# A routed feed-forward layer on one core: gate and up products two rounds behind the turned rows, and row copies moved to ScalarE

## The reference, cut to what matters

```python
y = einsum('bct,bcd->bdt', x, weights[itok])            # 1024 tokens x 256
probs = softmax(y @ w_router); top_w, top_i = top_k(probs, 4)
top_w = top_w / sum(top_w)
g = silu(y @ we1[e]) * (y @ we3[e]) * cw[:, e]          # 16 experts, 256 -> 128
moe_out = sum_e g @ we2[e]                              # 128 -> 256
shared = silu(y @ ws1) * (y @ ws3) @ ws2                # 256 -> 512 -> 256
out = x + shared / 5 + moe_out * 4 / 5
```

## Time and profile before

| | |
|---|---|
| time of the three executions | 149.14, 149.97, 151.33 us |
| the profiled execution: its span, first to last instruction | 167.7 us |
| mean granted TensorE clock | 0.983 of full speed |
| PE (matmul) busy | 139.6 us, 83%, 816 instructions |
| PE weight loads busy | 116.3 us, 69% |
| VectorE (DVE) busy | 101.4 us, 60% |
| ScalarE (ACT) busy | 67.7 us, 40% |
| GpSimd (POOL) busy | 66.7 us, 40% |
| DMA packets | 29.81 MB in 23741 packets |
| row copies `xt<-store_t` by DMA | 43 of 128 KB each |

### The profile page before, as it was taken

How to read it: one execution, slowest core, us unless ns; L and a number is a source line. 1 busy time by engine, 2 the same in 40 slices (tenths; PEclk the granted TensorE clock), 3 DMA queues, 4 the chain that set the end, 5 groups by cost and what they waited for, 6 DMA issues and landing times.

```text
span 167.7 us, 2807 instructions
## 1 busy us (share of the span) xinstructions
PE 139.6 (83%) x816; PEld 116.3 (69%) x816; DVE 101.4 (60%) x271; ACT 67.7 (40%) x158; POOL 66.7 (40%) x79
## 2 busy tenths in 40 slices
PE   6949999898789299989979388978989499996840
PEld 2419988686578189979969377967978378884730
DVE  1304699989299365577974487473746263116993
ACT  3004379992453333263332442285333221249200
POOL 0600000027747473654847174644737467200000
PEclk9999999999999969999999999999999999999997
DMA  1724889989354635666656333533522212299433
GB/s 32 253 63 126 262 263 335 296 286 335 110 178 131 190 125 158 207 201 192 190 170 220 146 125 127 189 119 132 199 86 96 94 63 98 81 373 418 195 121 125
DMA packets 23741, 29.81 MB, mean 178 GB/s; under 512 B 4112, under 2 KB 20496, under 8 KB 23600
## 3 DMA queue, kind: packets, MB, share of 16 engines
q1 hardware_dynamic: 19632, 19.86, 35.6%
q0 software_dynamic: 3120, 8.52, 15.4%
q10 hardware_dynamic: 976, 1.26, 2.3%
HBM read 17.58 MB, written 6.42 MB: 143 GB/s over the span
## 4 chain that ended last, share of the span: by engine, by line
PE 47%; DVE 14%; DMA 14%; ACT 8%; issue 7%; another core or an unknown queue 4%; POOL 3%; DVEq 1%; POOLq 1%; ACTq 0%; SPq 0%
PE up_ps L997 15%; PE down_ps L1013 11%; PE up_ps L991 6%; PE gate_ps L950 5%; PE down_ps L975 4%; DMA store_t<-y_of,token_i 3%; DMA itok_rows<-in_itok_B 2%; POOL result L451 2%; DMA raw<-result 2%; PE down_ps L854 2%; DVE acc L809 2%; ACT raw L566 2%; ACT gt L546 2%; DMA g<-in_L_cond_weights,cond_idx 2%
## 5 line engine op out<-in xcount | busy, mean ns | idle before, releaser
L444 POOL DMA_INDIRECT store_t<-y_of,token_i x32 | 32.6, 1018 | 48.3 <-DVE token_i L709 28.2
L451 POOL DMA_INDIRECT result<-store_t,back_i x32 | 31.2, 975 | 23.7 <-DVE store_t L791 16.3
L1013 PE MATMUL down_ps<-w,gt 128*128 x94 | 25.3, 391 | 11.9 <-ACT gt L546 9.7
L1013 PEld LDWEIGHTS down_ps<-w,gt 128*128 128x128 f32 x94 | 16.1, 189 | 15.6 <-issue 14.3
L791 DVE SCALAR_TENSOR_TENSOR store_t<-down_ps,valid,store_t 128x256 f32 x47 | 21.4, 456 | 8.6 <-DVE store_t L791 3.7
L997 PE MATMUL up_ps<-w_hi,x_hi 128*128 x78 | 23.7, 304 | 1.5 <-DVE x_lo L757 0.8
L762 DVE TENSOR_TENSOR g<-sil,up_ps 128x256 f32<-128x256 f32 (+1 forms) x24 | 9.9, 412 | 20.8 <-ACT sil L554 15.6
L554 ACT ACTIVATE sil<-up_ps 128x256 f32<-128x256 f32 (+1 forms) x24 | 9.2, 384 | 32.1 <-PE up_ps L997 18.4
L997 PE MATMUL up_ps<-w_hi,x_lo 128*128 x78 | 22.0, 282 | 0.0
L997 PE MATMUL up_ps<-w_lo,x_hi 128*128 x78 | 21.9, 281 | 0.0
L546 ACT ACTIVATE gt<-down_ps 128x256 f32<-128x256 f32 (+1 forms) x24 | 9.1, 379 | 22.6 <-PE down_ps L975 12.7
(11 more groups left out here) (153 smaller groups left out, 240.5 us busy)
## 6 DMA issues: line engine op xcount, KB each, us to landing
xt<-store_t SPq DMA_DIRECT2D x43, 128.0 KB
raw<-in_L_ffn_we SPq DMA_DIRECT2D x30, 128.0 KB, 3.4
w<-in_L_ffn_we SPq DMA_DIRECT2D x4, 512.0 KB
raw<-result SPq DMA_DIRECT2D x4, 512.0 KB, 5.0
w_lo<-result SPq DMA_DIRECT2D x4, 512.0 KB, 8.1
acc<-in_x SPq DMA_DIRECT2D x2, 512.0 KB, 5.7
y_of<-store_t ACTq DMA_DIRECT2D x1, 1024.0 KB, 6.0
out<-acc SPq DMA_DIRECT2D x3, 256.0 KB, 2.1
```

The source lines that it names most:

```text
L444: pool.indirect_dma_start(xs[:, j, :], None, y_of, bass.IndirectOffsetOnAxis(ap=token_i[:, j:j + 1], axis=0),).then_inc(tile_in[j % TT], 16)
L451: pool.indirect_dma_start(result, bass.IndirectOffsetOnAxis(ap=back_i[:, j:j + 1], axis=0), merged[:, j, :], None,).then_inc(result_out[j ...
L1013: last = pe.matmul(out_ps[b][:, h, :], gt[:, b, h, :], w2_of(experts[2 + h]), start=True, stop=True)
```

## The change

Gate and up products run two rounds behind the turned rows (`UP_LAG`), the gated rows are turned four rounds behind (`TURN_LAG`) and the second products five (`LAG`), so there are 29 rounds. `x_hi` and `x_lo` get three buffers (`XB`). In rounds 2 to 5 the turn of pair i stands behind the gate and up products of pair i-2. ScalarE copies the rows of all pairs; in round i it copies those of pair i+2, last in the round before `high(n)`. SyncE keeps only the four late weight loads. The ring for copied rows moves: three places in `store_t` for pairs 0 to 5, one in `w_2` for pair 6, then three in `raw`. A turn now waits on the buffers in PSUM itself (`t_x_hi`, `t_x_lo`). Of the shared steps, `gate_up` (4,0), (5,0), (4,1), (5,1) now stand in rounds 24 to 27, ahead of the second products of that round; `gated(4)` stands on VectorE in round 28, ahead of the last merge. `item_e_i` is laid out for the new distance of 3 rounds between gate and up and the second products.

```diff
@@ -41,7 +41,11 @@
     ITEMS_UP = 2 * PAIRS
     RESULTS = T * TOP_K
     RING = 3
-    LAG = 3
+    UP_LAG = 2
+    TURN_LAG = 4
+    LAG = 5
+    XB = 3
+    XT_RAW = 5
     SRING = 4
     WARM = 8
...
+        xt_early = [store_t[:, 10 + 2 * k:12 + 2 * k, :] for k in range(RING)]
+        xt_ring = [raw[:, XT_RAW + k, :].rearrange("p (i d) -> p i d", i=2) for k in range(RING)]
+
+        def xt_of(n):
+            if n < 2 * RING:
+                return xt_early[n % RING]
+            if n == 2 * RING:
+                return w_2[:, E:E + FRONT, :]
+            return xt_ring[(n - 1) % RING]
+
+        raw_at = ([xt_early[k].rearrange("p i d -> p (i d)") for k in range(FRONT)] + [raw[:, k, :] for k in range(E - LATE)]
+                  + [xt_early[FRONT].rearrange("p i d -> p (i d)")] + [raw[:, k, :] for k in range(4)])
...
-            registers = {}
-
-            def copy_pair(n):
-
...
-                if n >= RING:
-                    sp.wait_ge(t_turned, n - RING + 1)
-                else:
-                    sp.wait_ge(dve_lo, n + 1)
-                for i in range(halves(n)):
-                    j = 2 * n + i
-                    if j < TILES:
-                        sp.wait_ge(tile_in[j % TT], 16 * (j // TT + 1))
-                    sp.dma_start(xt[:, n % RING, i, :],
-                                 xs[:, bass.ds(registers[j], 1), :].rearrange("p a d -> p (a d)")).then_inc(xt_in[n % RING], 16)
-
-            for n in range(EARLY, PAIRS):
-                copy_pair(n)
-                if n in LOAD_BEHIND:
-                    load(LOAD_BEHIND[n])
+            for n in LOAD_BEHIND:
+                sp.wait_ge(t_turned, n - RING + 1)
+                load(LOAD_BEHIND[n])
...
+            registers = {}
+
+            def copy_pair(n):
+                if n % 6 == 0:
+                    some = range(2 * n, 2 * n + 12)
+                    values = [act.alloc_register(f"tile{j}") for j in some]
+                    act.wait_ge(items_done, 1)
+                    act.load(values, item_t_i[0:1, some[0]:some[-1] + 1])
+                    registers.update({j: act.snap(v, donate=True, min_val=0, max_val=TILES - 1) for j, v in zip(some, values)})
+                if n >= RING:
+                    act.wait_ge(t_turned, n - RING + 1)
+                    if n == 2 * RING:
+                        act.wait_ge(down_done, STEPS)
+                    if n == 2 * RING + 1:
+                        act.wait_ge(t_gate_up, PLAIN)
+                        act.wait_ge(dve_lo, max(turn[XT_RAW + FRONT + k] for k in range(RING)) + 1)
+                else:
+                    act.wait_ge(dve_lo, n + 1)
+                for i in range(halves(n)):
+                    j = 2 * n + i
+                    if j < TILES:
+                        act.wait_ge(tile_in[j % TT], 16 * (j // TT + 1))
+                    act.activation(xt_of(n)[:, i, :], xs[:, bass.ds(registers[j], 1), :].rearrange("p a d -> p (a d)"), ACT.Copy).then_inc(xt_out, 1)
+
             for n in range(EARLY):
...
+                copy_pair(n)
             for n in HI_BEHIND[-1]:
                 high(n)
+            def turned_high(n):
+                if n < PAIRS:
+                    b, c, m = n % 2, n % XB, halves(n)
+                    act.wait_ge(t_turned, n + 1)
+                    act.activation((x_hi[:, c, :, :] if n >= PLAIN else x_f[b])[:, 0:m, :], xt_ps[b][:, 0:m, :], ACT.Copy).then_inc(t_x_hi, 1)
+
             for i in range(PAIRS + LAG):
                 if i == 0:
                     act.wait_ge(g_done, STEPS)
                 if i == 1:
                     act.wait_ge(down_done, STEPS)
-                if (n := pair_at(i, LAG)) is not None:
+                if i >= UP_LAG + PLAIN:
+                    turned_high(i)
+                if (n := pair_at(i, TURN_LAG)) is not None:
                     b, m = n % 2, halves(n)
                     act.wait_ge(t_g_turned, n + 1)
                     act.activation(gt[:, b, 0:m, :], gt_ps[b][:, 0:m, :], ACT.Copy).then_inc(t_g_out, 1)
-                if (n := pair_at(i, 0)) is not None:
-                    b, m = n % 2, halves(n)
-                    act.wait_ge(t_turned, n + 1)
-                    act.activation((x_hi[:, b, :, :] if n >= PLAIN else x_f[b])[:, 0:m, :], xt_ps[b][:, 0:m, :], ACT.Copy).then_inc(t_x_hi, 1)
-                if (n := pair_at(i, 1)) is not None:
+                if (n := pair_at(i, UP_LAG)) is not None:
                     b, m = n % 2, halves(n)
                     act.wait_ge(t_gate_up, n + 1)
                     act.activation(t_sil[:, b, 0:m, :], gu_ps[b][:, 0:m, 0:H], ACT.Silu).then_inc(t_silu, 1)
+                if i < UP_LAG + PLAIN:
+                    turned_high(i)
+                if i + EARLY < PAIRS:
+                    copy_pair(i + EARLY)
...
+            def turned_low(n):
+                if PLAIN <= n < PAIRS:
+                    b, c, m = n % 2, n % XB, halves(n)
+                    dve.wait_ge(t_x_hi, n + 1)
+                    dve.tensor_tensor(x_lo[:, c, 0:m, :], xt_ps[b][:, 0:m, :], x_hi[:, c, 0:m, :].bitcast(F32),
+                                      ALU.subtract).then_inc(t_x_lo, 1)
+
             tiles = []
             for i in range(PAIRS + LAG):
-                if (n := pair_at(i, 0)) is not None and n >= PLAIN:
-                    b, m = n % 2, halves(n)
-                    dve.wait_ge(t_x_hi, n + 1)
-                    dve.tensor_tensor(x_lo[:, b, 0:m, :], xt_ps[b][:, 0:m, :], x_hi[:, b, 0:m, :].bitcast(F32),
-                                      ALU.subtract).then_inc(t_x_lo, 1)
-                if (n := pair_at(i, 1)) is not None:
+                if i >= UP_LAG + PLAIN:
+                    turned_low(i)
+                if (n := pair_at(i, UP_LAG)) is not None:
                     b, m = n % 2, halves(n)
                     dve.wait_ge(t_silu, n + 1)
                     dve.tensor_tensor(t_gated[:, b, 0:m, :], t_sil[:, b, 0:m, :], gu_ps[b][:, 0:m, H:2 * H], ALU.mult).then_inc(t_g, 1)
+                if i < UP_LAG + PLAIN:
+                    turned_low(i)
                 if i < 2:
...
+                if i == PAIRS + LAG - 1:
+                    gated(STEPS)
...
+                first = UP_LAG <= i < UP_LAG + PLAIN
+                if (n := pair_at(i, 0)) is not None and n and not first:
                     turn_pair(n)
-                if i > 1:
-                    experts = load_experts(i - 1)
+                if i > UP_LAG:
+                    experts = load_experts(i - UP_LAG)
+                if (n := pair_at(i, TURN_LAG)) is not None:
+                    turn_gated(n)
+                if (n := pair_at(i, UP_LAG)) is not None:
+                    gate_up_pair(n)
+                if first:
+                    turn_pair(i)
+                if PAIRS <= i < PAIRS + 2:
+                    pe.wait_ge(dve_lo, UNITS + 1)
+                    gate_up(STEPS + i - PAIRS, 0)
+                elif PAIRS + 2 <= i < PAIRS + 4:
+                    gate_up(STEPS + i - PAIRS - 2, 1)
                 if (n := pair_at(i, LAG)) is not None:
...
-            gate_up(STEPS, 1)
-            gate_up(STEPS + 1, 0)
-            gate_up(STEPS + 1, 1)
+                    down_pair(n)
+
+            pe.wait_ge(dve_lo, UNITS + 2)
+            gate_up(STEPS + 2, 0)
             down(STEPS)
...
+            gate_up(STEPS + 2, 1)
+            gate_up(STEPS + 3, 0)
+            pe.wait_ge(t_merged, ITEMS)
+            down(STEPS + 1)
+            gate_up(STEPS + 3, 1)
+            down(STEPS + 2)
+            down(STEPS + 3)
```

The functions `turn_gated`, `gate_up_pair` and `down_pair` hold the bodies that the loop had before, with `c = n % XB` for the buffers of `x_hi` and `x_lo`. `turn_pair` gained these waits:

```diff
+                b = n % 2
+                pe.wait_ge(xt_out, 2 * n + halves(n))
                 if n < 2:
                     pe.wait_ge(silu_done, STEPS - 1 + n)
+                elif n - 2 < PLAIN:
+                    pe.wait_ge(t_x_hi, n - 1)
+                else:
+                    pe.wait_ge(t_x_lo, n - 1 - PLAIN)
```

More of the change, by code:

```diff
@@ L89, in adaln_ffn @@
         acc = sb("acc", [P, TT, D])
-        itok_rows = sb("itok_rows", [P, 1], I32)
-        quarter_i = sb("quarter_i", [P, 1], I32)
-        cond_idx = sb("cond_idx", [P, 1], I32)
+        cond_i = sb("cond_i", [P, 3], I32)
+        itok_rows, quarter_i, cond_idx = (cond_i[:, k:k + 1] for k in range(3))
         early_exp = sb("early_exp", [P, 2])
@@ L107, in adaln_ffn @@
         gt = sb("gt", [P, 2, 2, P])
-        x_hi = sb("x_hi", [P, 2, 2, D], F32R)
-        x_lo = sb("x_lo", [P, 2, 2, D], F32R)
+        x_hi = sb("x_hi", [P, XB, 2, D], F32R)
+        x_lo = sb("x_lo", [P, XB, 2, D], F32R)
         top_d = sb("top_d", [P, TT, TOP_K])
@@ L252, in adaln_ffn @@
         xt_out = sem("xt_out")
-        xt_in = [sem(f"xt_in{r}") for r in range(RING)]
         t_cleared = sem("t_cleared")
@@ L772, in _ @@
                     dve.memset(merged[:, 2 * i:2 * i + 2, :], 0.0).then_inc(t_cleared, 1)
-                if i % 6 == 1 and (first := 2 * (i - 1)) < ITEMS_UP:
+                if i % 6 == UP_LAG + 1 and (first := 2 * (i - UP_LAG - 1)) < ITEMS_UP:
```

(80 more changed lines are left out.)

28 lines of the change are left out of this document (3 added, 25 removed).

## The result

The changed kernel took 156.86 us (median of 4: 155.90 to 158.98) beside 149.69 us: ratio 1.042, 95% interval 1.034 to 1.051. The ratio compares the fast executions only, those within 1.5% of the fastest of their kernel, and so is a little under 156.86 / 149.69 = 1.048. Slower, as forecast; 155.7 was predicted, with 147.0 to 158.0.

A forecast was written before the change was run, and what follows sets the result against it. TensorE's own instructions were taken to bound each steady round at 2.95 us. Late low parts -0.5, first rounds +2.5 and last rounds +3.7 made +5.7 us on 149.97, so 155.7 us, with a range of 147.0 to 158.0.

The forecast's parts named there:

- The reading of the span: Whole kernel: timed rounds take TensorE's 2.95 us; the profile's 19.2 us of late signals, waits and lowered clock nearly all its own.
- First rounds: TensorE's first turn of gated rows waits 2.8 us for gated(0), before 0.3: +2.5 us, bounds 0 to 3.
- late low parts: A late `x_lo` gets one more round of room from longer distance and three buffers: -0.5 us, between 0 and -0.8.
- Last rounds: More TensorE work ahead of pair 20's second products moves the last scatter: +3.7 us, bounds 3.0 to 5.5.
- Row copies: Row copies move from SyncE's transfers to ScalarE: saving hidden, 0 us; a gain of 3.8 kept as a rival.
- The clock: First rounds: the new wait slows TensorE's clock, products +1.2 us, turns about +0.4, 157.3 us; 0.10 together with blocked copies.

The follow-up runs named there:

- e1: The changed kernel with the second shared sums and the low parts of blocks 11 and 12 put behind gated(0) on VectorE; 1.017 of the kernel before.
- e8: The changed kernel with the low parts of blocks 13 and 14 also ahead of gated(0) on VectorE; turn of pair 1 to last scatter 84.9 us, from 83.4.
- After-third: The changed kernel, unedited, in a third profile; from the turn of pair 1 to POOL's start of the last scatter (A) 82.0 us.
- e4: The kernel before with only ScalarE copying every pair's rows, into the old ring; 1.003 of the kernel before.
- e2: The changed kernel with the shared products of steps 4 and 5 back where the kernel before has them; 1.019 of the kernel before.
- e3: The changed kernel with both edits, those of e1 and e2; 1.014 of the kernel before.
- after: The changed kernel, unedited, in its first profile; turn of pair 1 to last scatter 83.4 us, ratio 1.042 to the kernel before.

## Why the prediction was right

**The reading of the span: right.** Rounds at TensorE's pace, the late signals foreign to timed runs. All the sums rested on it.

**First rounds, +2.5, and late low parts, -0.5: mechanism right, net effect too large.** The wait worked out at 2.8 us measured 2.72, 2.0 and 2.7; e1 and e8 move it down and up, and the end follows. What it replaced was undersized: up to pair 20's second products the kernel before has in its two new profiles not 0.8 us of waits (0.3 + 0.5) but 2.3 to 2.5 (68.3 - 65.8), those for transfers among them. After-third has 3.1 (72.6, less 65.8 and the 3.7 of further work): the 2.7 and little else. So the two terms together were some +0.6 us and not +2.0. e4 shows that the waits for transfers went with the copies; which part of the change took the others isn't separated.

**Last rounds, +3.7: right for the shift.** 3.72 us of TensorE's work stand ahead of pair 20's second products, the seven scatters stayed closed, and from those products to the last scatter it is 9.4 us as before. But undoing the two shared halves alone gives 2.0 us back, not 2.8, for then POOL's pace sets the end (e2). The prediction looked at this pace for the last seven scatters only, not for those ahead of them.

**Row copies, 0: right** (e4). The 1.3 us of transfer waits in one profile of before lay between my bounds 0 and 3.8.

**The clock, given 0.10 as a rival: it happened in two of three profiles.** It costs 1.4 to 1.7 us, where the rival had 1.6. The sum without it, +5.7, was 1.3 us too large: after-third less before is +4.4 in A. The clock filled most of this gap, +5.3 (with a wait shorter by 0.7) and +5.7 in the other two. The median came out near the forecast partly by luck, because these two errors cancel. Measured by medians the difference is 7.2 us; the traces account for 4.4 to 5.7 of it, and how much of the rest is the clock in the front, which falls in some executions of both kernels, no run here separates.

## What to carry to other kernels

Where one engine's own instructions set the pace of every round, more distance between the stages gains only what it waits now, and each wait or piece of work put ahead of the last item of a chain moves the end in full, as long as the engine that finishes the chain has gaps. Where that engine is closed up, as POOL is in e2, its own pace sets the end. Before moving a step a round later, list what stands between its old and its new place on every queue: here two shared sums and two low parts stood there on VectorE. Work that already lies hidden beside the end of a kernel should stay there, and a profiled span that is far from the timed median should be explained before its waits are counted as gains.

## What the runs showed of the hardware

- One profiled execution in fourteen had signals from TensorE arriving up to 4.7 us late, with a span of 167.7 us where two others of the same kernel have 151.8 and 151.5.
- The granted clock is not a function of the wait alone: behind 2.7 us of idling it fell to 1.2 GHz in one execution of the changed kernel (0.66 granted in 55 to 60 us) and stayed at 2.4 GHz in another (1.00). The Trainium skill (TensorE: Matmul & The Clock Gate, "Loop structure matters more than you think") has long waits in the loop turn TensorE cold. Here that holds for three of six traces with waits of 2.0 to 4.0 us.
- Scatters of 128 rows of 1 KB follow each other on POOL every 1.28 us (0.97 busy, 0.30 between), however early their rows are merged (e2, e3).
- The front differs by such a stretch too: TensorE's turn of pair 1 starts at 49.13 us with a granted clock of 0.91 in 10 to 47 us (after) and at 46.03 with 1.00 in 10 to 46 (after, third). The two answers of the windows view:

```profile
10.00:47.00 37.00, 34.49 (x200) 28.64 (x199) 24.64 (x111) 22.06 (x47) 6.45 (x7) 0.91 0.75 228
```

```profile
10.00:46.00 36.00, 32.84 (x208) 27.55 (x208) 26.75 (x115) 22.98 (x50) 8.25 (x8) 1.00 0.78 241
```
